# In SyncE's order, the maxima of the next group ahead of the reciprocals of the previous one

## The chip, the cores and the metric

The kernel runs on one core of a Trainium2 chip. The metric is the device time of one execution in microseconds (us), the median of several. Engines are named as in the profile: PE is TensorE's matmuls, PEld its weight loads, DVE is VectorE, ACT ScalarE, POOL GpSimd and SP SyncE. SP computes nothing here: it issues every DMA of the kernel, in program order, and waits on semaphores between them. All of them go through one hardware queue (q1 in the profile).

## The reference

A "macaron" block over x of shape (8, 1024, 256), float32:

```python
x = x + 0.5 * ffn(layernorm(x))        # feed-forward with blockwise FP4 quantized inputs and weights, 256 -> 704 -> 256
x = x + attention(layernorm(x))        # 16 heads of 16 columns, causal
x = x + 0.5 * ffn(layernorm(x))

# attention, for each of 8 sequences of 1024 rows
logits = einsum('bhqd,bhkd->bhqk', q, k) * 16 ** -0.5      # above the diagonal: -max float
e = exp(logits - max(logits)); attn = e / sum(e)
out = einsum('bhqk,bhkd->bhqd', attn, v)                   # then @ Wo.T
```

Only the softmax part of the attention concerns the change: the maximum of each row of logits, the exponentials, the weighted sum of the values, and the division by the sum of the exponentials.

## The kernel before

The program runs `feed_forward(0)`, `project_qkv()`, `attention()` and `feed_forward(1)` one after the other, each with a stream of instructions for each engine. The change touches `attention()` alone.

`attention()` works through 32 groups: 8 sequences (`BATCH`) times 4 groups of 4 heads (`GROUPS`, `GROUP`). The loops are written out. Group n = b * GROUPS + g keeps its q, k and v in slot g % 4 of a ring of four buffers (`RING`). q and k are split into three bf16 parts each, stacked to 96 partitions (`STACK`). Two more partitions (`STACK_MAX` = 98) of `q_stack` hold the maximum of each row in two bf16 parts, against -1.0 in `k_stack`: so the matmul of the scores gives logits minus maximum.

Within a group PE, ACT, POOL and DVE go through ten steps (`NS`), i = 0 to 9:

- PE (`score_head`, L1308 and the mask at L1313) makes the scores of a step in `hT_ps` and `av_ps`, and then the values of the step before (`values`, L1332). The values of step 9 are made in step 0 of the next group. Between them stand "units" (`max_unit`, L1291): scores of a later group without maxima, from which only the maxima are taken. PE starts a group after `pe.wait_ge(max_loaded[...])`, the arrival of that group's maxima in `q_stack`.
- ACT takes the exponentials (L1413, L1418). It copies the sums of the first three steps out to `o_sb` at step 3 (half 0), and those of the last seven in step 0 of the next group (half 1): `copy_out`, L1396. It waits for the half before to have been sent from `o_sb`.
- DVE reduces the units to maxima. In step 6 (`MAX_STEP`) it finishes those of the next group; PE turns them (L1298), ACT casts the high part (`m_hi`, L1389) and in step 7 DVE makes the low part (`m_lo`, L1511), both in `mT`. After step 4 it takes the reciprocals of the previous group's sums (`one_over`, L1520).
- POOL masks the blocks on the diagonal of four steps (`causal`, L1448), and after the last of them multiplies the previous group's output by its reciprocals (`divide`, L1456), which waits for both loads of `load_group`.

SP's order in group n is that of the function `group` in its block: `send_half(n - 1, 1)`; `load_sums(n - 1)`; `fill(n + 3)`, 13 DMAs (L789 to L792) that load q, k and v of the group three ahead; `send_out(n - 2)`; `send_half(n, 0)`; `load_group(n - 1)`; `send_max(n + 1)`.

`load_group` writes the reciprocals to DRAM (L1205), waits for them to have landed, spreads them (L1208), loads the output (L1213), waits for the spread and loads it (L1216). `send_max` waits for `mT`, writes it to DRAM (L1178), waits for it to have landed and loads it into `q_stack` (L1181). Group 0 has no previous group and so no `load_group`. Groups 29 to 31 have no `fill`, and group 31 has no `send_max`.

Of the kernel before, what the change touches and what calls it, by code (L numbers as in the profile page):

```python
# [67 lines left out]
def build(nc, x_in, wq_in, wk_in, wv_in, wo_in, wg_in, wu_in, wd_in, y_out):  # L68
    V, S, G, T = nc.vector, nc.scalar, nc.gpsimd, nc.tensor
    top = ExitStack()  # L70
    with top:
# [706 lines left out]
        def fill(sp, b, g):  # L778

            r = g % RING  # L780
            qs, ks, vs = ring[r]
            cols = bass.ds(b * SEQ, SEQ)
            q, k = (p[:, g * GROUP * DH:(g + 1) * GROUP * DH, cols].rearrange("a (h d) t -> a d h t", d=DH)
                    for p in qk_parts)
            at = 0

            for part, times in ((0, 3), (1, 2), (2, 1)):
                for n in range(times):
                    sp.dma_start(qs[at:at + DH, :, :], q[part]).then_inc(stack_loaded[r], 16)  # L789
                    sp.dma_start(ks[at:at + DH, :, :], k[n]).then_inc(stack_loaded[r], 16)  # L790
                    at += DH
            sp.dma_start(vs[:, :, :, :].rearrange("p t h d -> p t (h d)"),  # L792
                         v_ones[bass.ds(b * SEQ_TILES, SEQ_TILES), :, g * GROUP:(g + 1) * GROUP, :]
                         .rearrange("t p h d -> p t (h d)")).then_inc(stack_loaded[r], 16)
# [255 lines left out]
        def attention():  # L1050
# [71 lines left out]
            with ExitStack() as ctx:  # L1122
# [18 lines left out]
                def once(eng, name, n, k):  # L1141

                    value = n + k
                    if isinstance(value, int) and value <= 0:
                        return
                    eng.wait_ge(s[name], value)

                def groups(eng, group):

                    for b in range(BATCH):  # L1150
                        for g in range(GROUPS):
                            group(b, g, b == BATCH - 1)
# [3 lines left out]
                def later(b, g, ahead, last):  # L1156

                    if last and g + ahead >= GROUPS:
                        return None
                    return b + (g + ahead) // GROUPS, (g + ahead) % GROUPS  # L1160

                def before(b, g):

                    if g:
                        return b, g - 1
                    return None if isinstance(b, int) and b == 0 else (b - 1, GROUPS - 1)

                with nc.Block() as block:
                    @block.sync
                    def _(sp):  # L1170
                        def send_max(b, g):

                            r = g % RING
                            n = b * GROUPS + g
                            once(sp, "m_lo", n, 1)
                            once(sp, "m_hi", n, 1)
                            slot = max_rows[bass.ds(n, 1), :, :].rearrange("o a c -> (o a) c")
                            sp.dma_start(slot.rearrange("a (u q) -> u a q", q=P), mT[:, :, :]  # L1178
                                         ).then_inc(s["m_stored"], 16)
                            sp.wait_ge(s["m_stored"], n * 16 + 16)  # L1180
                            sp.dma_start(ring[r][0][STACK:STACK_MAX, :, :].rearrange("p h t -> p (h t)"), slot  # L1181
                                         ).then_inc(max_loaded[r], 16)

                        def send_half(b, g, j):

                            n = b * GROUPS + g
                            once(sp, "o_sb", n * 2 + j, 1)
                            sp.dma_start(o_all[n, j, :, :], o_sb[:, :]).then_inc(s["o_sent"], 16)
                            sp.dma_start(sum_rows[n, j, :, :], o_sb[DH:P:VPAD, :]).then_inc(s["o_sent"], 16)

                        def load_sums(b, g):

                            n = b * GROUPS + g
                            sp.wait_ge(s["o_sent"], 64 * (n + 1))
                            once(sp, "inverse", n, 0)
                            sp.dma_start(sums[:, :], sum_rows[n, :, :, :].rearrange("j h (q c) -> (j h q) c", c=PER_ROW)
                                         ).then_inc(s["sums"], 16)
                            sp.dma_start(o_rows[n, :, :, :], o_all[n, :, :, :].rearrange("j (h r) c -> (j h) r c", r=VPAD)
                                         [:, 0:DH, :]).then_inc(s["o_packed"], 16)

                        def load_group(b, g):

                            n = b * GROUPS + g
                            once(sp, "inverse", n, 1)
                            sp.dma_start(inverse_rows[n, :, :].rearrange("a (q c) -> (a q) c", c=PER_ROW), inverse[:, :]  # L1205
                                         ).then_inc(s["inverse_sent"], 16)
                            sp.wait_ge(s["inverse_sent"], 16 * (n + 1))
                            sp.dma_start(inverse_all[n, :, :, :], inverse_rows[n, :, :].unsqueeze(1)  # L1208
                                         .broadcast_to([2 * GROUP, DH, CHUNK])).then_inc(s["inverse_spread"], 16)
                            if n:  # L1210
                                sp.wait_ge(ao_stored, 32 * n)
                            sp.wait_ge(s["o_packed"], 16 * (n + 1))
                            sp.dma_start(o_group[:, :], o_rows[n, :, :, :].rearrange("a d c -> (a d) c")  # L1213
                                         ).then_inc(s["o_loaded"], 16)
                            sp.wait_ge(s["inverse_spread"], 16 * (n + 1))
                            sp.dma_start(o_inverse[:, :], inverse_all[n, :, :, :].rearrange("a d c -> (a d) c")  # L1216
                                         ).then_inc(s["o_loaded"], 16)

                        def send_out(b, g):

                            n = b * GROUPS + g
                            once(sp, "ao", n, 1)
                            for j in range(2):
                                at = b * SEQ + j * CHUNK
                                sp.dma_start(attn_cols[g * GROUP * DH:(g + 1) * GROUP * DH, at:at + CHUNK],
                                             o_group[j * GROUP * DH:(j + 1) * GROUP * DH, :]).then_inc(ao_stored, 16)
# [6 lines left out]
                        def group(b, g, last):  # L1233
                            n = b * GROUPS + g
                            prev, nxt = before(b, g), later(b, g, 3, last)
                            if prev:
                                send_half(*prev, 1)
                                load_sums(*prev)
                            if nxt:
                                once(sp, "pv", n * NS, 0)  # L1240
                                fill(sp, *nxt)
                            if prev and before(*prev):
                                send_out(*before(*prev))
                            send_half(b, g, 0)
                            if prev:
                                load_group(*prev)
                            nxt = later(b, g, 1, last)
                            if nxt:
                                send_max(*nxt)

                        groups(sp, group)
                        send_half(*LAST, 1)
                        load_sums(*LAST)
# [323 lines left out]
```

## Time and profile before

| | |
|---|---|
| time, median of 3 runs | 2431.79 us (2428.57 to 2432.48) |
| the profiled execution: its own time | 2434.77 us |
| its span, first to last instruction | 2433.0 us |
| mean granted TensorE clock | 0.920 |
| PE busy | 2088.9 us (86%) |
| DVE busy | 1919.4 us (79%) |
| ACT busy | 1291.1 us (53%) |
| POOL busy | 1037.4 us (43%) |
| DMA queue q1, share of 16 engines | 36.9% |

Times within the profile are us from the start of the span. Idle time of an engine is put down to what released it. Rows of SP are the issue of a DMA, not its transfer: between two rows SP issues or waits. [...] The DMA share is the mean busy share of 16 DMA engines; it can pass 1 a little.

### The profile page before, as it was taken

How to read it: one execution, taken by the hardware profiler on the slowest of the kernel's cores; microseconds unless marked ns; L12 is line 12 of the kernel's file. 1: busy time of each engine (PE TensorE's matmuls, PEld its weight loads, DVE VectorE, ACT ScalarE, POOL GpSimd, SP SyncE). 2: the span in 40 equal slices, each digit the busy share in tenths (PEclk: the TensorE clock that was granted, in tenths of full speed). 3: DMA queues.
4: the chain of work that ended last, by engine and by line, in shares of the span. 5: the costliest groups of instructions: out<-in, count | busy, mean ns of one | idle time of the engine just before them, and what ended most of it. 6: DMA issues, size and time to landing. Idle time of an engine off the chain costs nothing. (4 is left out here: it accounts for less than half of the span.)

```text
span 2433.0 us, 44426 instructions
## 1 busy us (share of the span) xinstructions
PE 2088.9 (86%) x13448; PEld 1350.7 (56%) x13448; DVE 1919.4 (79%) x4327; ACT 1291.1 (53%) x2221; POOL 1037.4 (43%) x1639
## 2 busy tenths in 40 slices
PE   3899999979989878778787787787879579999998
PEld 3788888868843323223232232232323568888887
DVE  6899999969878667667676676776765479999996
ACT  3455555427627556556565565655658235555553
POOL 4788888836540111011111111101111058888885
PEclk7899999989979889889898898988989789999999
DMA  6000000006885556465565564655642500000000
GB/s 192 1 0 0 0 0 0 0 13 233 241 174 88 91 97 112 94 108 98 94 110 97 102 108 93 113 93 95 112 94 78 153 17 18 22 17 22 17 22 23
DMA packets 163503, 184.92 MB, mean 76 GB/s; under 512 B 57696, under 2 KB 109280, under 8 KB 163040
## 3 DMA queue, kind: packets, MB, share of 16 engines
q1 hardware_dynamic: 163360, 183.17, 36.9%
q8 instruction: 71, 1.16, 0.2%
q14 instruction: 72, 0.59, 0.1%
HBM read 113.90 MB, written 85.98 MB: 82 GB/s over the span
## 5 line engine op out<-in xcount | busy, mean ns | idle before, releaser
L1413 ACT ACTIVATE probs<-hT_ps 128x512 f32<-128x512 f32 (+3 forms) x320 | 273.7, 855 | 373.2 <-PE hT_ps L1313 293.3
L1448 POOL TENSOR_SCALAR_AFFINE_SELECT diag_scores<-diag_scores 128x256 f32<-128x256 f32 (+1 forms) x192 | 94.5, 493 | 846.7 <-ACT diag_scores L1411 842.9
L1308 PE MATMUL hT_ps<-q_stack,k_stack 98*128 98x512 bf16 (+3 forms) x768 | 243.1, 346 | 189.1 <-DMA q_stack<-max_rows 188.7
L1291 PE MATMUL gu_ps<-k_stack,q_stack 96*128 96x512 bf16 (+3 forms) x994 | 322.5, 360 | 15.1 <-DVE part_max L1491 8.9
L1332 PE MATMUL gu_ps<-probs,v_group 128*17 128x512 f32 (+3 forms) x3072 | 326.8, 514 | 2.2 <-ACT probs L1413 1.1
L708 PE MATMUL gu_ps<-wguT_hi,ffn_xT_hi 128*128 128x512 f32 (+1 forms) x768 | 313.9, 409 | 7.5 <-DVE ffn_xT_lo L584 5.1
L1491 DVE CUSTOM_DVE_ANT_0 gu_ps<-gu_ps,mask_qk 128x256 f32<-128x256 f32 x510 | 283.4, 582 | 28.6 <-PE gu_ps L1291 21.5
L1496 DVE TENSOR_REDUCE part_max<-gu_ps 128x1 f32<-128x512 f32 x352 | 233.4, 686 | 77.6 <-PE gu_ps L1291 77.5
L708 PE MATMUL gu_ps<-wguT_hi,ffn_xT_lo 128*128 128x512 f32 (+1 forms) x768 | 290.8, 379 | 0.0
L708 PE MATMUL gu_ps<-wguT_lo,ffn_xT_hi 128*128 128x512 f32 (+1 forms) x768 | 290.3, 378 | 0.0
L1413 ACT ACTIVATE probs<-av_ps 128x512 f32<-128x512 f32 (+3 forms) x320 | 275.4, 861 | 14.0 <-PE av_ps L1313 14.0
L686 ACT ACTIVATE ffn_z<-xs,ffn_shift,ffn_rstd 128x256 f32 (+1 forms) x128 | 77.0, 602 | 350.4 <-POOL ffn_shift L637 350.3
L1291 PEld LDWEIGHTS gu_ps<-k_stack,q_stack 96*128 96x128 bf16 x994 | 99.8, 105 | 281.9 <-DVE part_max L1491 132.0
L1308 PEld LDWEIGHTS hT_ps<-q_stack,k_stack 98*128 98x128 bf16 x768 | 75.7, 101 | 254.4 <-DMA q_stack<-max_rows 196.4
L607 POOL TENSOR_TENSOR ffn_hq<-ffn_g_h,ffn_nscale 128x704 f32<-128x704 f32 (+1 forms) x256 | 210.5, 843 | 2.2 <-DVE ffn_g_h L571 2.2
L1308 PE MATMUL av_ps<-q_stack,k_stack 98*128 98x512 bf16 (+3 forms) x768 | 209.8, 345 | 1.8 <-ACT probs L1413 1.4
L739 PE MATMUL xd_ps<-wdT_hi,ffn_hT_hi 128*128 128x256 f32 x640 | 191.7, 299 | 21.4 <-DVE ffn_hT_lo L523 21.4
L656 POOL TENSOR_TENSOR ffn_v_h<-ffn_h,ffn_rec 128x704 f32<-128x704 f32 x128 | 178.1, 1392 | 17.0 <-DVE ffn_rec L567 7.4
L739 PE MATMUL xd_ps<-wdT_hi,ffn_hT_lo 128*128 128x256 f32 x640 | 181.9, 284 | 0.0
L739 PE MATMUL xd_ps<-wdT_lo,ffn_hT_hi 128*128 128x256 f32 x640 | 181.7, 284 | 0.0
L1483 DVE TENSOR_TENSOR gu_ps<-gu_ps,mask_qk 128x512 f32<-128x512 f32 x33 | 23.1, 699 | 198.2 <-PE gu_ps L1291 198.2
L1291 PE MATMUL xd_ps<-k_stack,q_stack 96*128 96x512 bf16 (+3 forms) x542 | 163.6, 340 | 6.2 <-DVE part_max L1486 2.1
(207 smaller groups left out, 5229.5 us busy)
## 6 DMA issues: line engine op xcount, KB each, us to landing
q_stack<-q_parts SPq DMA_DIRECT2D x192, 128.0 KB, 7.4
k_stack<-k_parts SPq DMA_DIRECT2D x192, 128.0 KB, 8.1
o_all<-o_sb SPq DMA_DIRECT2D x64, 256.0 KB
q_parts<-qkv_parts SPq DMA_DIRECT2D x32, 384.0 KB, 2.7
k_parts<-qkv_parts SPq DMA_DIRECT2D x32, 384.0 KB, 2.8
v_ones<-qkv_vst SPq DMA_DIRECT2D x16, 544.0 KB, 3.8
v_group<-v_ones SPq DMA_DIRECT2D x32, 272.0 KB, 11.7
xs<-in_L_attn_x SPq DMA_DIRECT2D x8, 1024.0 KB, 12.1
```

Of the source, the lines that this page charges most:

```text
L607: last = G.tensor_tensor(blocks(hq[:, to:to + n]), blocks(g_h[:, of:of + n]), spread(nscale[:, par, of // BLK:(of + n) // BLK]), ALU.mult)
L656: G.tensor_tensor(blocks(v_h[:, par, :]), blocks(h[:]), spread(rec[:, OF_H]), ALU.mult).then_inc(s["v_h"], 1)
L686: S.activation(z[:, 1 - par, :], x_tile(i + 5), ACT.Identity, bias=shift[:], scale=rstd[:]).then_inc(s["z"], 1)
L708: last = T.matmul(gu_ps[:, n, 0:cols.stop - cols.start], x[:, buf, k * P:(k + 1) * P], w[:, k, cols], start=k == 0 and m == 0, stop=k == K ...
L739: T.matmul(down_ps, x[:, k * P:(k + 1) * P], w[:, k, :], start=k == 0 and n == 0, stop=False)
L1291: mm = T.matmul(out[:, e, :], qs[0:STACK, h0 + e, t * P:(t + 1) * P], ks[0:STACK, h0 + e, c * CHUNK:c * CHUNK + w], start=True, stop=True)
L1308: mm = T.matmul(scores[pair][:, e, at:at + w], ks[0:STACK_MAX, h, t * P:(t + 1) * P], qs[0:STACK_MAX, h, (j + 1) * CHUNK - w:(j + 1) * CHUNK],
L1332: mm = T.matmul(o_ps[h * VPAD:h * VPAD + VCOLS, CHUNK - w:CHUNK], vs[:, t, h, :], probs[:, h // 2, i % 2, h % 2, at:at + w], start=first, ...
L1413: S.activation(probs[:, pair, i % 2, :, first:w], scores[pair][:, :, first:w], ACT.Exp, scale=DH ** -0.5).then_inc(s[pr], 1)
L1448: G.affine_select(out=block_of, in_=block_of, compare_op=ALU.is_ge, fill=MASKED, base=0, pattern=[[0, 2], [0, count], [1, P]], channel_mul ...
L1491: last = V.tensor_tensor_reduce(out=ps[:, e * w:(e + 1) * w], in0=ps[:, e * w:(e + 1) * w], in1=mask_qk[:, CHUNK - w:CHUNK], scale=1.0, sc ...
L1496: last = V.tensor_reduce(part_max[:, h0:h0 + per, t, c], ps[:, 0:per * w].rearrange("p (h w) -> p h w", h=per), AX.X, ALU.max)
```

## The change

Two statements of SP's `group` trade places: `send_max` of the next group now comes before `load_group` of the previous one. What each issues and waits for is as before. No other engine's program changes.

```diff
                             if prev and before(*prev):
                                 send_out(*before(*prev))
                             send_half(b, g, 0)
-                            if prev:
-                                load_group(*prev)
                             nxt = later(b, g, 1, last)
                             if nxt:
                                 send_max(*nxt)
+                            if prev:
+                                load_group(*prev)
```

## Rows read from the trace of the kernel before

**Rows 1.** Waits of PE, 758 to 1808 us: waited for, total, times, longest.
```profile
PE hT_ps L1308 <- DMA q_stack<-max_rows: 181.2, 27, 7.7
```
**Rows 2.** Stretches: group 29, group 1 until PE stops, groups 1 to 28 together.
```profile
core 0: us, PE busy (x) PEld busy (x) DVE busy (x) ACT busy (x) POOL busy (x), PEclk, DMA share, GB/s
...
1808.38:1839.13 30.75, 29.89 (x206) 11.16 (x207) 25.42 (x70) 21.41 (x35) 4.20 (x7) 0.92 0.21 63
...
758.58:787.13 28.55, 27.69 (x206) 10.51 (x204) 26.17 (x72) 21.84 (x36) 2.96 (x6) 1.00 0.68 104
758.58:1808.38 1049.80, 837.93 (x5742) 312.33 (x5740) 740.92 (x1990) 610.74 (x981) 118.02 (x196) 0.90 0.60 101
```
**Rows 3.** SP's timeline in group 12: start, duration of the issue.
```profile
1213.88 0.34 SPq L1188 DMA_DIRECT2D o_all<-o_sb  x1
...
1216.03 0.33 SPq L1196 DMA_DIRECT2D sums<-sum_rows  x1
...
1226.53 0.58 SPq L1188 DMA_DIRECT2D o_all<-o_sb  x1
...
1227.73 0.44 SPq L1205 DMA_DIRECT2D inverse_rows<-inverse  x1
1236.40 0.70 SPq L1208 DMA_DIRECT2D inverse_all<-inverse_rows  x1
...
1240.24 0.33 SPq L1216 DMA_DIRECT2D o_inverse<-inverse_all  x1
1240.67 1.16 SPq L1178 DMA_DIRECT2D max_rows<-mT  x1
1243.26 0.25 SPq L1181 DMA_DIRECT2D q_stack<-max_rows  x1
```
**Rows 4.** Timeline of POOL, DVE and PE in group 12 and at group 13's start.
```profile
1222.68 0.42 POOL L1448 TENSOR_SCALAR_AFFINE_SELECT diag_scores<-diag_scores 128x256 f32<-128x256 f32 x1 [15.16 <-ACT diag_scores L1411]
...
1232.26 0.27 DVE L1511 TENSOR_TENSOR mT<-gu_ps,mT 32x128 bf16<-32x128 f32 x1
...
1245.39 0.61 PE L1308 MATMUL hT_ps<-q_stack,k_stack 98*128 98x512 bf16 x1 [6.56 <-DMA q_stack<-max_rows]
```
**Rows 5.** Timeline of PE, SP and DVE in group 1.
```profile
758.58 0.38 PE L1308 MATMUL hT_ps<-q_stack,k_stack 98*128 98x512 bf16 x1
762.17 0.35 SPq L1188 DMA_DIRECT2D o_all<-o_sb  x1
780.56 0.27 DVE L1511 TENSOR_TENSOR mT<-gu_ps,mT 32x128 bf16<-32x128 f32 x1
784.19 0.70 SPq L1208 DMA_DIRECT2D inverse_all<-inverse_rows  x1
```
**Rows 6.** SP's timeline in group 28, the last with a fill.
```profile
1777.16 0.34 SPq L1188 DMA_DIRECT2D o_all<-o_sb  x1
...
1800.20 0.70 SPq L1208 DMA_DIRECT2D inverse_all<-inverse_rows  x1
```
**Rows 7.** Stretches at the end of group 12 and the start of group 13.
```profile
1235.50:1236.00 0.50, 0.50 (x8) 0.00 (x0) 0.50 (x3) 0.43 (x2) 0.43 (x2) 1.00 0.18 33
...
1243.00:1244.00 1.00, 0.00 (x0) 0.00 (x0) 0.00 (x0) 0.00 (x0) 0.88 (x1) 0.66 0.00 0
...
1249.00:1250.00 1.00, 1.00 (x8) 0.07 (x8) 0.69 (x1) 0.62 (x1) 0.00 (x0) 0.50 0.00 0
```
**Rows 8.** The answers on inverse_rows (first) and on o_inverse (second).
```profile
DMA to landing us min/median/max: 1.4/9.6/10.6
...
DMA to landing us min/median/max: 2.5/2.7/3.0
```
**Rows 9.** The maxima of group 0: SP's timeline, and a stretch with the DMA share.
```profile
720.70 0.31 SPq L1178 DMA_DIRECT2D max_rows<-mT  x1
726.14 0.30 SPq L1181 DMA_DIRECT2D q_stack<-max_rows  x1
...
724.00:724.50 0.50, 0.46 (x2) 0.10 (x1) 0.50 (x3) 0.00 (x0) 0.00 (x0) 0.50 0.08 18
```

## The prediction

> **What bounds the kernel now.** I read the page's groups of instructions first: among the costly ones the scores of `hT_ps` stand out, since PE is idle before them on a DMA, the maxima of the group. The waits of PE in the attention show the size: 181.2 us in 27 group starts, 6.7 us each, with nothing near it [rows 1]. The start at 1808.38 lies just outside that window, so 28 starts have such a gap: those of groups 2 to 29. Group 1 starts without one, as do 30 and 31.
>
> The stretches give the turn of a group. Groups 1 to 28 take 1049.80 us, 37.49 each [rows 2]. Group 1 started at a granted clock of 1.00 and PE had work for 28.55 us before it stopped; group 29 started at half clock, had no gap after it and took 30.75 [rows 2]. So a turn is 28.6 us of work, about 2.2 us from the low clock at its start, and 6.7 us of gap: 37.5. The low clock follows from the gap: PE stops at 1238.83 (6.56 us before 1245.39), the clock is going down between 1243 and 1244, and it is still at 0.50 between 1249 and 1250, four microseconds into the next group [rows 4, 7].
>
> What the gap is made of stands in SP's timeline of group 12 [rows 3]. The maxima are ready at 1232.53 (DVE's low part) [rows 4]. SP is then inside `load_group`: it issued the store of the reciprocals at 1227.73 and waits until 1236.40 for it to land, since the 13 fills and the outputs, issued since the sums' load at 1216.03, are still in the queue. In the same answer the share of the DMA engines falls to 0.18 only at 1235.5 [rows 7]. Then come the spread and the loads, and SP gets to the maxima at 1240.67, loads them at 1243.26, and PE starts 2.13 us after that issue.
>
> **The change, part by part.** No instruction is added or taken away; both blocks issue what they did.
>
> *Removed from the path.* From the landing of the backlog (1236.40) to the load of the maxima (1243.26) it is 6.86 us [rows 3]. In the new order SP stands at `send_max` from about 1227.7, waits for `m_lo` until 1232.5, and issues the store. That store is behind the same backlog. How soon after it does it land? The nearest row is the reciprocals' store, which sets SP free at 1236.40, about 0.9 us after the DMA share falls. The store of group 0's maxima, issued at 720.70 into a backlog, was less quick: the share was down to 0.08 at 724.0 to 724.5, and the load follows at 726.14 [rows 9], about 2.1 us after 724.0, so 1.2 more. I take 0.4 us more than the reciprocals, with 0 and 1.2 as ends.
>
> *Moved behind.* `load_group` now begins after the load of the maxima, at t0. Counted from t0: issue 0.3; the store of the reciprocals lands in 1.4 to 1.5, the minimum over the kernel, reached when the queue is empty [rows 8]; from the spread to the issue of the last load 3.84 [rows 3], and 0.4 for that issue. SP is free at t0 + 6.0. PE has started at t0 + 2.13, and half 1 of the output is ready 3.59 us after a start at full clock (762.17 less 758.58) [rows 5], so at t0 + 5.7. SP is 0.3 us late for it. The clock loss that hid this (2.2 us) is gone.
>
> *A collision.* The load of `o_inverse` (256 KB) is issued 0.4 us ahead of `o_all` on the same queue; SP waits for `o_all` to land before it issues the sums and the fills: 2.15 us today [rows 3]. `o_inverse` alone takes 2.7 us to land [rows 8]. The addition is between 0 and those 2.7; I take 0.9, a third, since most of the 2.7 is not transfer: the 2.15 of a transfer of the same size and 2.7 hold one latency each, and only the bytes queue.
>
> *Unchanged.* From half 1 to the end of the backlog: 22.02 in group 1 (784.19 less 762.17), 22.52 in group 12, 23.04 in group 28 [rows 5, 3, 6]. Over the 28 groups with this pattern the mean is 23.1, between 22.0 and 24.1. The same DMAs are in it.
>
> *The new turn*, from t0 to t0: 6.0 + 0.9 + 23.1 + 0.4 = 30.4 us. The same sum for today's order, 2.1 + 3.6 + 2.2 + 23.1 + 6.9 = 37.9, is 0.4 above the 37.49 measured, so this way of adding is good to about that. PE's work is 28.55, so a gap of 1.85 us stays, still on the maxima. DVE is busy 26.17 of those 28.55 us, and its low part comes 22.25 us after the start (780.83 less 758.58) [rows 5], 4 us before the backlog ends: it doesn't decide.
>
> *What waits for the moved block.* POOL's `divide` waits for `o_inverse`: landed at t0 + 8.3, divided by t0 + 9.6, that is 7.5 us after PE's start. POOL's first mask, at 1222.68, comes 8.8 us after half 1 at 1213.88 [rows 3, 4]; with 3.6 from a start at full clock to half 1 that is 12.4, so 4.9 us of cover. If that cover went, every microsecond would go to ACT and PE. `send_out` and `one_over` ask for the result even later. ACT's next copy to `o_sb`, at step 3, asks for half 1 to have been sent, which it has been before the fills are issued.
>
> *The sum.* 28 turns, 37.49 less 30.4, are 198.5 us. Group 29 starts at full clock, another 2.2. Groups 29 to 31 have no gap and no backlog, and gain nothing else. 2434.8 less 200.7 is 2234.1 for the profiled execution; it ran 3.0 us over the median shown, so **2231 us** for a median.
>
> **Rivals.**
>
> *A: the forecast*, SP's turn through the backlog stays the bound, at 29.5 to 31.4 us: 2206 to 2259. 50%.
>
> *B: PE becomes the bound.* The maxima arrive before PE is through, and the turn is 28.55. 28 times 8.94 is 250, with the 2.2 it gives 2179. It needs 1.9 us less than A's turn: no collision, and a store of the maxima that lands ahead of the tail of the backlog. The queue's tail (the outputs of group n) is in fact issued ahead of the maxima, and the reciprocals' 9.6 us speak against it. 20%. [...]
>
> *C: the clock stays low.* The gap of 1.85 us is shorter than the 4 us and more that the clock held out above, but it comes every turn. Half 1 would be ready at t0 + 2.1 + 5.8 = 7.9, well behind `o_inverse`; the turn is 7.9 + 0.2 + 23.1 + 0.4 = 31.6, the gain 5.9 a turn, and group 29 gains nothing more: 165 us, 2267. 12%. [...]
>
> *D: the collision is large.* The deferred loads and the new group's output hold each other up by the full 2.7, and the store takes the full 1.2: 6.0 + 2.7 + 23.1 + 1.2 = 33.0, a gain of 4.5 a turn, 128 us with the 2.2, giving 2304. 11%.
>
> *E: slower.* One mechanism: the reciprocals' store takes its 9.6 us, the median [rows 8], by itself, not for the backlog. Then SP, which was covered by the backlog in today's order, is free only at t0 + 14.2; the next group's output, sums and fill stand behind it, and the turn is 38.6, 1.1 over today's: 31 us more, 2463. It decides from a chain of 13.1 us instead of 6.0. For it: 28 of the 32 stores took 8 us or more. Against: the minimum of 1.4, and that the median matches the backlog. 4%.
>
> *F: it does not do what it says*: another wait of the same length takes the gap (SP held by `m_lo`, say), and the time stays near 2432. Against it, `m_lo` comes 4 us before it could matter [rows 5]. 3%.
>
> **Numbers.** A measurement of this kernel can tell 0.2%, about 5 us, from no change. Faster by more: A, B, C, D, 93%. Within: F, 3%. Slower: E, 4%. The range goes from B's 2179, a little below for its own error, to 2295, which holds C and the lower part of D; outside are E, F, and most of D.
>
> **What would show each step.** In the changed profile SP's load of the maxima should come straight after the store's wait, some 27 us after PE's start, with the spread after it; the wait of PE on the maxima should fall from 6.7 to about 2 us a group, the turn of groups 2 to 28 to 30.4; the clock in the attention should go from 0.90 to nearly 1.00. The landing of `inverse_rows` should fall from a median of 9.6 to 1.4 to 2, that of `max_rows` be 4 or 5. From `o_all` (half 1) to the sums it should be 3 us instead of 2.15. No wait of PE on the maxima is B, a clock of 0.5 at the group starts C, a gap over 4 us D. The prediction is wrong if POOL's `divide` or SP's `o_sb` wait shows up on ACT's path, or if the backlog itself gets longer than 24 us.

## The result, and the profile after

The changed kernel takes 2238.97 us (median of 4 runs, 2234.38 to 2242.09), the kernel before 2430.22 us (median of 4 runs): a ratio of 0.9211, 95% interval 0.9191 to 0.9231. The forecast was 2231, the range from a little below 2179 to 2295.

First the page of the changed kernel: the span, the busy time of the engines, and the scores' group with its idle time and what ended it.

```profile
span 2238.9 us, 44426 instructions
...
PE 2045.1 (91%) x13448; PEld 1336.8 (60%) x13448; DVE 1914.3 (86%) x4327; ACT 1289.7 (58%) x2221; POOL 1037.8 (46%) x1639
...
L1308 PE MATMUL hT_ps<-q_stack,k_stack 98*128 98x512 bf16 (+3 forms) x768 | 232.7, 333 | 40.2 <-DMA q_stack<-max_rows 39.6
```

PE's wait for the maxima is 39.6 us over the kernel. Within groups 1 to 28 of the attention it is what answers to [rows 1]:

```profile
PE hT_ps L1308 <- DMA q_stack<-max_rows: 39.4, 18, 4.1
```

18 of the 28 starts, those of groups 2 to 29, have a gap and 10 have none or one of 0.12 us; on average over 28 it is 1.4 us, where it was 6.7. The stretches answer to [rows 2]; the columns are the same. The first is groups 1 to 28, the second group 1 alone, then a turn that starts at full clock and one that starts at half.

```profile
754.53:1615.64 861.11, 797.16 (x5742) 299.60 (x5740) 735.97 (x1990) 608.85 (x981) 117.10 (x195) 0.97 0.73 123
754.53:782.93 28.40, 27.54 (x207) 10.53 (x206) 26.01 (x72) 21.69 (x36) 2.96 (x6) 1.00 0.65 98
1336.99:1367.85 30.86, 27.70 (x206) 10.52 (x206) 27.03 (x73) 22.08 (x36) 4.23 (x7) 1.00 0.72 123
1212.69:1244.02 31.33, 30.46 (x206) 11.34 (x207) 25.56 (x70) 21.41 (x35) 4.22 (x7) 0.90 0.70 121
```

The 28 turns take 861.11 us, 30.75 each, against 37.49: 188.7 us. Group 29 starts at full clock and takes 28.40 instead of 30.75. The rest of the 194.1 us between the spans lies outside: group 1 starts 4.05 us earlier, at 754.53, before anything that changed, and the tail from group 30 on is 1.0 us longer.

SP's timeline of that turn (group 20) and the start of the next answers to [rows 3].

```profile
1341.05 0.43 SPq L1188 DMA_DIRECT2D o_all<-o_sb  x1
...
1344.28 0.31 SPq L1196 DMA_DIRECT2D sums<-sum_rows  x1
...
1354.63 0.58 SPq L1188 DMA_DIRECT2D o_all<-o_sb  x1
...
1359.29 0.33 SPq L1178 DMA_DIRECT2D max_rows<-mT  x1
1365.77 0.26 SPq L1181 DMA_DIRECT2D q_stack<-max_rows  x1
1366.07 0.34 SPq L1205 DMA_DIRECT2D inverse_rows<-inverse  x1
1368.00 0.71 SPq L1208 DMA_DIRECT2D inverse_all<-inverse_rows  x1
...
1371.75 0.32 SPq L1216 DMA_DIRECT2D o_inverse<-inverse_all  x1
1372.81 0.32 SPq L1188 DMA_DIRECT2D o_all<-o_sb  x1
```

The reader is to see three things. The maxima's store is issued as soon as DVE has made them (22.3 us after the start) and then stands 6.5 us in the queue: it now waits for the fills' backlog, as the reciprocals' store did. The reciprocals' store lands in 1.9 us behind it. And SP gets from the load of the maxima to the next half 1 in 7.0 us.

The landing times of the two small stores have changed places; inverse_rows first, then max_rows (the landing of the store).

```profile
DMA to landing us min/median/max: 1.7/1.8/3.2
...
DMA to landing us min/median/max: 1.4/5.6/8.5
```

PE around the start at 1367.85, and behind it the stretches of the next microseconds, with the granted clock in the third column from the end:

```profile
1367.85 0.39 PE L1308 MATMUL hT_ps<-q_stack,k_stack 98*128 98x512 bf16 x1 [2.31 <-DMA q_stack<-max_rows]
```
```profile
1368.00:1369.00 1.00, 1.00 (x10) 0.64 (x9) 0.43 (x1) 0.16 (x1) 0.00 (x0) 1.00 0.00 0
1369.00:1370.00 1.00, 1.00 (x6) 0.35 (x3) 0.97 (x3) 0.96 (x2) 0.00 (x0) 0.57 0.27 72
1370.00:1371.00 1.00, 1.00 (x5) 0.15 (x8) 1.00 (x2) 0.92 (x1) 0.00 (x0) 0.50 0.86 201
1371.00:1372.00 1.00, 1.00 (x8) 0.00 (x0) 0.18 (x1) 0.00 (x0) 0.00 (x0) 0.50 0.74 268
1372.00:1373.00 1.00, 1.00 (x9) 0.53 (x6) 0.29 (x1) 0.58 (x1) 0.00 (x0) 0.72 0.29 35
```

A gap of 2.31 us is followed by the low clock too, but late: PE works again from 1367.85, the clock is still 1.00 until 1369, and then 0.50 for over three microseconds. In 10 of the 28 turns DVE's low part comes 23.8 us or more after the start instead of 22.3, the two turns of these rows among them (from 1212.69 and from 1367.85). These 10 are the ones at low clock: in each of them the granted clock is at 0.50 for a part of the first 8 us, and in none of the others.

### The profile page after: what moved, and what is told of

Read it like the earlier page. It is cut to its first block and busy times, and to the rows that moved or that the text cites. A ratio compares the mean times of both kernels' runs of the same rounds, so it can differ in the third digit from the quotient of the medians.

```text
span 2238.9 us, 44426 instructions
## 1 busy us (share of the span) xinstructions
PE 2045.1 (91%) x13448; PEld 1336.8 (60%) x13448; DVE 1914.3 (86%) x4327; ACT 1289.7 (58%) x2221; POOL 1037.8 (46%) x1639
## 3 DMA queue, kind: packets, MB, share of 16 engines
q8 instruction: 71, 1.16, 0.2%
## 5 line engine op out<-in xcount | busy, mean ns | idle before, releaser
L1291 PE MATMUL gu_ps<-k_stack,q_stack 96*128 96x512 bf16 (+3 forms) x994 | 312.0, 346 | 15.3 <-DVE part_max L1491 8.7
L1332 PE MATMUL gu_ps<-probs,v_group 128*17 128x512 f32 (+3 forms) x3072 | 318.7, 503 | 2.2 <-ACT probs L1413 1.1
L1491 DVE CUSTOM_DVE_ANT_0 gu_ps<-gu_ps,mask_qk 128x256 f32<-128x256 f32 x510 | 283.1, 581 | 30.4 <-PE gu_ps L1291 23.4
L1308 PE MATMUL hT_ps<-q_stack,k_stack 98*128 98x512 bf16 (+3 forms) x768 | 232.7, 333 | 40.2 <-DMA q_stack<-max_rows 39.6
L1291 PEld LDWEIGHTS gu_ps<-k_stack,q_stack 96*128 96x128 bf16 x994 | 93.9, 99 | 267.5 <-DVE part_max L1491 132.5
L1308 PE MATMUL av_ps<-q_stack,k_stack 98*128 98x512 bf16 (+3 forms) x768 | 200.1, 332 | 1.8 <-ACT probs L1413 1.4
L1456 POOL TENSOR_TENSOR o_group<-o_group,o_inverse 128x512 f32<-128x512 f32 x32 | 40.8, 1274 | 334.9 <-DMA o_inverse<-inverse_all 334.9
L708 PEld LDWEIGHTS gu_ps<-wguT_hi,ffn_xT_hi 128*128 128x128 f32 x768 | 146.6, 191 | 27.0 <-DVE ffn_xT_lo L584 7.4
```

The lines of the kernel that those rows point to most:

```text
L708: last = T.matmul(gu_ps[:, n, 0:cols.stop - cols.start], x[:, buf, k * P:(k + 1) * P], w[:, k, cols], start=k == 0 and m == 0, stop=k == K ...
L1291: mm = T.matmul(out[:, e, :], qs[0:STACK, h0 + e, t * P:(t + 1) * P], ks[0:STACK, h0 + e, c * CHUNK:c * CHUNK + w], start=True, stop=True)
L1308: mm = T.matmul(scores[pair][:, e, at:at + w], ks[0:STACK_MAX, h, t * P:(t + 1) * P], qs[0:STACK_MAX, h, (j + 1) * CHUNK - w:(j + 1) * CHUNK],
L1332: mm = T.matmul(o_ps[h * VPAD:h * VPAD + VCOLS, CHUNK - w:CHUNK], vs[:, t, h, :], probs[:, h // 2, i % 2, h % 2, at:at + w], start=first, ...
L1491: last = V.tensor_tensor_reduce(out=ps[:, e * w:(e + 1) * w], in0=ps[:, e * w:(e + 1) * w], in1=mask_qk[:, CHUNK - w:CHUNK], scale=1.0, sc ...
```

## The experiments

The first theory was that of the prediction: a turn is SP's way through the queue, from half 1 through the fills' backlog to the maxima and, behind them, through the deferred block to the next half 1; PE's own 28.4 us come next. The rivals are named in each expectation.

**1. Is the order itself the gain, or what stood in the queue? thin_before and thin_after**

```diff
-                    sp.dma_start(qs[at:at + DH, :, :], q[part])
-                    sp.dma_start(ks[at:at + DH, :, :], k[n])
+                    sp.dma_start(qs[at:at + DH, 0:H, 0:W], q[part][:, 0:H, 0:W])
+                    sp.dma_start(ks[at:at + DH, 0:H, 0:W], k[n][:, 0:H, 0:W])
...
```

> The kernel before with fills that move 1/16 of the q and k bytes and 1/8 of those of v from group 4 on (later sequences compute on the data of the first). As many DMAs are issued. Theory: the order of the two blocks cost 6.9 us a turn only because the store of the reciprocals stood behind the fills' backlog. With the backlog gone SP reaches the maxima some 24 to 25 us after the start, the turn is 28.5 to 29.3, and the time 2175 to 2200. Rival: the reciprocals' block costs its time by itself in that order: above 2300.

> The changed kernel with the same thin fills (later sequences compute on the data of the first). Theory: PE is the bound, turn 28.5, 2172 to 2180, so within 1% of the kernel before with thin fills, where with full fills the two orders differ by 8%. Rival (the order itself is the gain): thin_before is slower by 5% or more.

Not shown in this diff: H and W are 4 heads and 1024 rows in the first sequence, 1 head and 256 rows in the later ones, and the load of v is thinned in the same way, to 1 of 8 tiles. So the kernel leaves out most of q, k and v of the later sequences; the instructions of all engines are as many as before.

Measured: thin_before 2179.56 us (2 runs, 0.8973 of the kernel before, 0.8946 to 0.8999), thin_after 2175.89 (2 runs, 0.8957, 0.8933 to 0.8981). The intervals overlap. The waits of PE in thin_before, the old order, from 750 us to 1560; they start with the largest:

```profile
PE gu_ps L1299 <- DVE part_max L1492: 12.7, 29, 0.4
PE gu_ps L1292 <- DVE part_max L1492: 7.6, 29, 0.3
```

No wait for the maxima is left in it, and its reciprocals' store lands in a median of 1.7 us where it took 9.6 [rows 8]. The turns are 28.52 and 28.46. So the order costs its 6.7 us a turn only while the full fills are in the queue: the same 13 issues with few bytes, and with fewer pieces, make it free. The gain of the change is the removal of a wait that the backlog stretched, not of work.

**2. Does the deferred block lie on the path? two_stores**

```diff
+                            sp.dma_start(inverse_rows[n]..., inverse[:, :]).then_inc(s["again"], 16)
+                            sp.wait_ge(s["again"], 16 * (n + 1))
                             sp.dma_start(inverse_rows[n]..., inverse[:, :]).then_inc(s["inverse_sent"], 16)
```

> The changed kernel with the reciprocals stored twice, one after the other with a wait for each: one more landing of 1.8 us in the deferred block. Theory: the block stands ahead of the next group's half 1, so the turn grows by it, less what the turns with a late half 1 (low clock, 5 to 6 us after the start, about 10 of 28) hide: 1.2 to 1.8 us a turn, 34 to 50 us, 2273 to 2289. Rival: the deferred block is hidden and the turn is the backlog's alone: 2239.

Measured: 2265.12 us (4 runs), ratio 0.9368 (0.9353 to 0.9382). In microseconds that is 26 over the changed kernel; by the ratios it is 1.7%, some 38 us, since the kernel before ran at 2416.49 on the chip of this comparison. The time in microseconds is below the 2273 to 2289 expected. In the profiles the turn is 31.60 against 30.75, 0.85 more, less than the 1.2 to 1.8 expected. The rival (no change) falls: the block is on the path. By stretches, as means over groups 2 to 27: SP is through with the block 1.5 us later, and from the load of the maxima to half 1 it is 7.9 us instead of 6.8; so 0.3 us are hidden where half 1 comes late anyway, since the turns at low clock grow by 0.5 us there and the others by 1.5. From half 1 to the sums it is 3.2 us instead of 3.0. Another 0.4 us is missing between the sums and the next load of the maxima, 20.6 instead of 21.1; why that stretch is shorter stays open.

**3. Take one wait out of it: store_first, and again**

```diff
                             send_half(b, g, 0)
+                            if prev:
+                                send_inverse(*prev)
                             nxt = later(b, g, 1, last)
                             if nxt:
                                 send_max(*nxt)
                             if prev:
                                 load_group(*prev)
```

`send_inverse` is the store of the reciprocals alone; `load_group` keeps the wait for it and all that follows.

> As the changed kernel, but the store of the reciprocals (16 KB) is issued ahead of the maxima and so lands in the backlog; the rest of that block stays behind the maxima. Theory: SP's stand in the deferred block, 6 us after the load of the maxima, sets half of the turns; without the wait for the store it is 4.2, the output no longer waits for SP and half of the collision with the load of the reciprocals goes too: turn 29.4 to 29.8 instead of 30.8, 2200 to 2212. Rival: the turn is set by the backlog alone and half 1 is late by the low clock: 2235 to 2240.

> store_first once more, beside v_behind on the same chip: 0.905 to 0.908 of the kernel before, whichever theory holds. It is there to tell 1% between the two.

Measured: 2199.08 us (4 runs), 0.9055 (0.9032 to 0.9078); the second time 2199.40 us (5 runs), 0.9049 (0.9033 to 0.9064). That is 1.7% under the changed kernel, and just below what was expected. SP in its group 20 and the next half 1:

```profile
1331.20 0.33 SPq L1178 DMA_DIRECT2D max_rows<-mT  x1
1336.32 0.26 SPq L1181 DMA_DIRECT2D q_stack<-max_rows  x1
1336.62 0.71 SPq L1212 DMA_DIRECT2D inverse_all<-inverse_rows  x1
...
1340.41 0.33 SPq L1220 DMA_DIRECT2D o_inverse<-inverse_all  x1
1341.78 0.32 SPq L1188 DMA_DIRECT2D o_all<-o_sb  x1
```

SP is through with the block at 1340.74 and now waits for half 1, which comes at 1341.78, where it had been SP that came late. In 27 of the 28 turns (in both profiles) half 1 is sent 3.6 us after the start, that is at full clock, and the gap before the maxima is still there but small:

```profile
PE hT_ps L1315 <- DMA q_stack<-max_rows: 15.2, 22, 2.3
```

The turn is 29.15, of which 28.6 are PE's. The gaps are 0.5 us on average, and no turn starts at a low clock (in the second profile one does). Against the changed kernel it is 1.2 us less from the load of the maxima to half 1 (5.6 instead of 6.8) and 0.7 less from there to the sums (2.3 instead of 3.0), as the theory had it.

**4. A queue of its own for the maxima: act_queue**

```diff
                                 if i == MAX_STEP and nxt:
                                     m_hi(*nxt, max_bank)
+                                if i == MAX_STEP + 1 and nxt:
+                                    store_max(act, *nxt)
+                                if i == MAX_STEP + 2 and nxt:
+                                    load_max(act, *nxt)
...
```

Not shown in this diff: SP calls `send_max` for group 0 alone.

> The maxima are stored and loaded from ACT's hardware queue (store after ACT's step 7, load after step 8) instead of SP's; SP's order is otherwise that of the changed kernel. Theory: what is left of the gap (about 1.5 us a turn of 30.8) is the place in SP's queue behind the fills; on a queue of its own the store lands early, PE becomes the bound at 28.4 to 28.6 us a turn, the clock stays at 1.00, and the time is 2170 to 2180. Rival: the 16 DMA engines are busy through that stretch whatever the queue, and the store lands with the backlog as before: 2239 or a little less. A third way: the two issues cost ACT 0.4 us each on PE's path: 2190 to 2200.

Measured: 2214.21 us (4 runs), 0.9110 (0.9087 to 0.9133): 1.1% under the changed kernel, far from 2170. The theory that the place in SP's queue was the trouble falls. First the landing of the stores, then ACT after its wait:

```profile
DMA to landing us min/median/max: 1.4/4.6/6.1
```
```profile
1166.90 0.25 ACTq L1181 DMA_DIRECT2D q_stack<-max_rows  x1
1167.25 1.02 ACT L1414 ACTIVATE probs<-hT_ps 128x1024 f32<-128x1024 f32 x1 [1.39 <-DMA max_rows<-mT]
```

On its own queue the store still takes 4.6 us, beside 5.6 in the changed kernel and 1.4 there for the store issued at 748.4, ahead of which the DMA share is 0.00 for two microseconds. The nearer comparison is store_first, where the reciprocals' store is ahead in the backlog too: there the maxima's store goes through SP's queue and lands 21.3 us after the issue of the sums' load (mean over groups 1 to 28), and from ACT's queue it lands 21.3 us after it as well. The queue of its own brought the landing forward by nothing, so its place in SP's queue is not what holds the store. The DMA engines are busy for most of that time: in the turn above the store is issued at 1161.84, the DMA share is 1.35 from 1162 to 1163, 1.16 and 0.67 in the next two microseconds and down to 0.02 from 1166, and the load is issued at 1166.90. The wait moved into ACT's stream, in front of the exponentials of the last step, 1.39 us in this turn and 21.0 us in 16 turns together. So what this version gained over the changed kernel is not an earlier landing; most likely it comes with the reciprocals' store, which went back into the backlog as in store_first. Beside store_first (0.9055 in the same comparison) it is 0.6% slower. How much of that is ACT's wait is not separated in this run.

**5. Fewer bytes ahead of the maxima: outputs_behind**

```diff
-                            if prev and before(*prev):
-                                send_out(*before(*prev))
-                            send_half(b, g, 0)
...
+                            if prev:
+                                spread_inverse(*prev)
+                            if prev and before(*prev):
+                                send_out(*before(*prev))
+                            send_half(b, g, 0)
                             if prev:
                                 load_group(*prev)
```

> As store_first, and the outputs (two attn_cols of 128 KB, o_all of 256 KB for half 0) are issued after the load of the maxima, between the spread of the reciprocals and the load of the output. Theory: store_first's turn of 29.2 us is the backlog ahead of the maxima's store; 512 KB less in it are 1.4 us at the 350 to 400 GB/s of its tail, more than the 0.6 us of gap left, so PE is the bound at 28.4 to 28.6 and the time is 2176 to 2186. What could spoil it: SP's stand after the load of the maxima grows by 3 us to about 5.3, still just under the 5.7 at which half 1 is ready. Rival: it passes that, half 1 is late again, turn 29.5 or more, 2205 or more. Second rival: the backlog's length is set by the fills alone, and nothing changes from 2199.

Measured: 2200.09 us (5 runs), 0.9104 (0.9091 to 0.9117). The theory (2176 to 2186) falls. In microseconds this is store_first's 2199.08, and the turn is 29.21 against 29.15; as a ratio it is 0.6% more, but the kernel before took 2416.49 us beside this one and 2428.97 beside store_first, so whether it is slower at all is not shown. What spoiled it is what the first rival names, at less than its price (2205 or more): half 1 is late. SP in its turn from 1132.57:

```profile
1159.53 0.25 SPq L1181 DMA_DIRECT2D q_stack<-max_rows  x1
1159.83 0.68 SPq L1212 DMA_DIRECT2D inverse_all<-inverse_rows  x1
1160.56 1.16 SPq L1233 DMA_DIRECT2D attn_cols<-o_group  x2
1161.76 0.59 SPq L1188 DMA_DIRECT2D o_all<-o_sb  x1
...
1164.24 0.34 SPq L1221 DMA_DIRECT2D o_group<-o_rows  x1
1164.63 0.92 SPq L1224 DMA_DIRECT2D o_inverse<-inverse_all  x1
1166.92 0.32 SPq L1188 DMA_DIRECT2D o_all<-o_sb  x1
```

From the load of the maxima to half 1 it is 7.4 us in this turn and 6.5 on average, not 5.6, and from there to the sums 3.0, not 2.3: SP now also waits for the outputs to land before it may load the next ones over them (40.1 us in 30 times in its waits). Over groups 2 to 27 the stretch from the sums to the load of the maxima is 19.8 us instead of 21.3, 1.5 shorter, as expected; but the sums are issued 7.4 us after the start instead of 5.9. What was taken from one side of the maxima came back on the other.

**6. The right bytes: v_behind**

```diff
                                 once(sp, "pv", n * NS, 0)
-                                fill(sp, *nxt)
+                                fill(sp, *nxt, with_v=False)
...
                             sp.dma_start(inverse_all[n]...)
+                            fill_v(sp, *far)
```

The second hunk is in `load_group`; the rest is store_first.

> As store_first, and the fill's load of v (272 KB in pieces of 272 bytes, 1 of 13 DMAs) is issued after the load of the maxima, right behind the spread of the reciprocals, where the queue is nearly empty. Theory: the turn of store_first, 29.2, is the backlog ahead of the maxima's store; at the 120 GB/s of the fills' stretch the load of v is some 2 us of it, more than the 0.6 us of gap; nothing is added to what SP waits for (the spread is ahead of it), so PE is the bound, 28.4 to 28.6 a turn, 2176 to 2186, 1% under store_first. Rival: the load of v delays half 1 and the sums behind it in the queue by as much as it frees: 2195 to 2210.

Measured: 2177.38 us (5 runs), 0.8957 of the kernel before (0.8945 to 0.8969), 1.0% under store_first on the same chip. The waits of PE in its attention, largest first, and SP from the store of the maxima to the next half 1:

```profile
PE gu_ps L1317 <- DVE part_max L1510: 12.8, 29, 0.4
PE gu_ps L1310 <- DVE part_max L1510: 7.7, 29, 0.3
```
```profile
1321.10 0.32 SPq L1185 DMA_DIRECT2D max_rows<-mT  x1
1324.22 0.26 SPq L1188 DMA_DIRECT2D q_stack<-max_rows  x1
...
1325.28 0.46 SPq L799 DMA_DIRECT2D v_group<-v_ones  x1
...
1327.89 0.32 SPq L1229 DMA_DIRECT2D o_inverse<-inverse_all  x1
1330.79 0.32 SPq L1195 DMA_DIRECT2D o_all<-o_sb  x1
```

The maxima are loaded 25.4 us after the start instead of 27.2, the wait for them is gone but for one of 0.3 us, the turn is 28.55, and the time is that of thin_after: with all its bytes the kernel runs as if the fills had nearly none. The stretch from the sums to the load of the maxima is 19.7 us instead of the 21.2 of store_first on the same chip: 272 KB of v in pieces of 272 bytes were worth 1.6 us in it, and the 512 KB of the outputs in experiment 5 were worth 1.5. So what a transfer ahead of the maxima costs does not go by its bytes. It is the best version of the study, 10.4% under the kernel before. PE is the bound in it: 770.29 of 795 us busy from 755 on, at a clock of 1.00.

## Why the prediction was right

*The bound and its composition* were right. PE waited for the maxima, SP stood in `load_group` because of the backlog (thin_before shows that the block is harmless without it), and the low clock followed from the gap: 0.90 over groups 1 to 28 with gaps of 6.7 us, 0.97 with gaps of 1.4.

*The turn* was forecast at 30.4 us and is 30.75. By its terms, as means over groups 2 to 27:

| term | forecast | measured |
|---|---|---|
| load of the maxima to half 1 | 6.0 | 6.8 |
| collision: half 1 to the sums, over 2.13 before the change | 0.9 | 0.9 |
| half 1 to the end of the backlog 23.1, the maxima's store after it 0.4 | 23.5 | 23.2 |
| sum | 30.4 | 30.9 |

The third term is measured as one stretch: from the sums to the load of the maxima it is 21.1 us, and before the change it was 21.0 from the sums to the landing of the reciprocals. So the maxima's store lands with the backlog as theirs did, and the 0.4 us between them did not come. The 0.9 us of the collision were the author's estimate: how much of the 2.7 us of `o_inverse` is transfer, no run shows; what the profiles show is 3.03 us from half 1 to the sums instead of 2.13. The 28 turns average 30.75, as the table leaves out the shorter groups 1 and 28.

*The mis-sized term is the first.* SP's stand was counted at 6.0 us with half 1 ready at 5.7. In the turns at full clock that is 0.3 us short: SP is through with the block 6.3 us after the load, since the reciprocals' store lands in 1.85 us on average and not in the kernel's minimum of 1.4 to 1.5, and half 1 goes out 6.3 us after the load (5.9 to 6.9; 3.7 to 5.1 after the start). In the other 10 half 1 is sent 5.0 to 6.1 us after the start, 7.5 after the load, as PE is slow in the first steps: a matmul of the scores (98x512) is 0.61 us from 1212.69, at a clock of 0.50, and 0.39 from 1336.99, at 1.00, while ACT's exponentials (128x1024) take 1.02 us in both turns and wait for PE. So rival C is no rival but part of A: it had 12% as the state of all turns, and the kernel is in it in 10 of 28. Whether a gap of 1.85 us costs the clock was open before the result. The runs show that gaps of 1.7 to 4.1 us are followed by it in 10 cases, and that others of up to 2.3 us, as the one before 813.75, are not. What tells them apart stays open. The price was small: a low start sends half 1 1.2 us later after the load than a start at full clock, but half 1 then stands further behind the load of `o_inverse`, and from half 1 to the sums it is 2.3 us instead of 3.5. The turns from a low start take 30.95 us on average, the others 30.78. In 8 of the 10 the gap behind them is gone too (0.12 us at most), since PE's work is then 30 us and more instead of 28.4; behind the other two it is 1.1 and 2.1 us.

*Why that is not more than 8 us in the time*: 28 times 0.35 are 10 us, and the 4 us that the profiled execution won ahead of the attention take a part of it back; the tail adds 1. That makes the 6.7 us by which the profiled execution (2240.77) is over the 2234.1 forecast for it.

*Rival B*, PE as the bound, did not happen, but its time of 2179 is that of v_behind (2177) and of the two thin kernels: the price was right, the condition was missing. The maxima's store, which it needed ahead of the tail of the backlog, takes 5.6 us, and its landing falls where the backlog ends (21.1 us after the sums, where the reciprocals landed 21.0 after them). *D* put the collision at 2.7, which was also named as its upper end; it is 0.9 on average and 2.9 at most (5.04 from half 1 to the sums in the group from 844.32). *E* needed a reciprocals' store that is slow by itself; it lands in 1.8 us. (Its chain of 13.1 us should read 14.2, the sum that stands before it; the turn of 38.6 is worked out from 14.2.) *F* needed another wait; there is none. The cover of POOL's `divide` was enough: 27 of its waits for `o_inverse` are 290.9 us in total, and none of ACT's or PE's waits names it.

*The signs that were named* came in the main: the reciprocals' landing went from 9.6 to 1.8, the clock in groups 1 to 28 from 0.90 to 0.97, the sums from 2.1 to 3.0 after half 1. The gap became 1.4 us instead of 2. Two were told too low. The landing of `max_rows` was to be 4 or 5 us and is 5.6. Its load was to come some 27 us after PE's start and comes at 28.8; the prediction's own turn of 30.4 less 2.1 gives 28.3, so the 27 did not follow from its sum. The limit of 24 us for the backlog was kept: 23.2 without the collision.

## What to carry to other kernels

In this kernel a wait for a small transfer lasted as long as the DMA work that was issued ahead of it, 9.6 us behind full fills and 1.7 behind thin ones, and a transfer from another queue fared no better (21.3 us after the sums from either). A transfer that another engine starts its next piece of work on should not stand behind such a wait. Moving it ahead gives back the wait; what then comes behind it (here the reciprocals) is the next thing to look at, first for waits that can be covered by issuing early (1.7%), then for transfers that nobody needs before the critical one (another 1.0%). Moving transfers that somebody does wait for gave nothing, nor did a second queue give an empty one.

## What was not expected of the hardware

The clock falls after the gap, not only in it: PE stopped at 1365.54, worked again from 1367.85, and was at 0.50 from just after 1369 until past 1372. A gap of 2.31 us thus slowed work that had begun more than a microsecond before. Of the 10 starts at low clock in the changed kernel, 6 went down after PE had resumed (0.7 to 1.3 us after) and 4 in the gap.

The clock can also fall without such a gap. In group 25 of the changed kernel it is at 0.50 from 1515.91, 22.6 us after a start behind a gap of 0.12 us, and v_behind has two such stretches, of some 3.5 us from 1262.5 and from 1378.5, though PE waits for the maxima in none of its turns but one, for 0.3 us. The longest stop of PE in the 12 us before each of them is 0.44 us. What brings it about stays open.

A store of 16 KB on ACT's hardware queue, while SP's queue was full, landed no earlier than the same store in SP's queue: 21.3 us after the sums in both.
